# Attention heads with maxima first, split row products, single banks and a reciprocal in quarters

## The chip, the cores and the metric

The kernel runs on one core of one Trainium2 chip. The metric is the device time of one execution in microseconds (us); the median of 3 runs of the kernel before is 5199.88 us (5199.38 to 5200.64).

PE is TensorE (PEld its weight loads), DVE is VectorE, ACT is ScalarE, POOL is GpSimd. PSUM has 8 banks of 128 x 512 f32; products land there, and DVE and ACT read them.

## The reference, cut to what matters

Eight layers run one after the other on x of 2048 tokens and 512 features. The change touches the fifth, a softmax attention over the 2048 tokens as one sequence:

```
q = (x @ Wq.T + bq) * cos(rot);  k = (x @ Wk.T + bk) * sin(rot);  v = x @ Wv.T + bv    # 16 heads of 32
scores = q @ k.T / sqrt(32) * spiral_weight[head]
attn   = softmax(scores, axis=-1)
out    = (attn @ v) @ Wo.T + bo
```

The kernel takes the maximum of each row of scores, adds its negative to the scores, takes the exponential, and divides the product with v by the sum of the exponentials.

## The kernel before, in words

`attention_heads` (tiles named attc) begins when q, k and v are in SBUF. Heads are handled in DT = 4 groups of QH = 4; the four heads of a group lie in the four groups of 32 partitions of q and k, so that a product of head h uses only rows 32h to 32h+31 of the PE array and products of different heads can run side by side. The 2048 queries of a group are cut into TC = 4 blocks of NB = 512, the keys into TT = 16 pieces of 128. A **unit** U is one piece of keys for one block of queries and all four heads: 16 units make a block, 64 a group (UNITS), 256 all (ALL). Units 192 to 255 (from LAST_GROUP on) are the last group.

In a unit of the first three groups PE does, in two halves (lines 1501 to 1508):

- `scores` of two heads: a row product (L1444, bf16), which writes the negative maxima of the queries into the bank (`ones16` by `rows`), and onto it the product of k and q (L1447, f32, which runs as two passes). The result is keys by queries. There are three banks for it, taken in turn: `score_bank(n)` waits until exponential n-3 is done.
- `maxima` of the other two heads of the **next** group (L1455, f32, two passes): queries by keys, one product of 128 queries and 512 keys for each head. DVE reduces both heads at once (L1558, 128x1024 to 128x2). There are two pairs of banks, 3 and 4, 5 and 6; `take` waits until DVE is done with the use before the last.
- `values` of the unit two before (LAG = 2), one half of the queries: L1468, prob by v, in the four column groups of 32 of the array, all 128 rows. They sum in bank 7 over a block.

ACT takes the four exponentials of a unit (L1534) from the score banks into `prob`, which has NP = 4 slots. Slot U is free again when the values of U-4 are done and its part in the sum of exponentials is taken. That sum is formed by POOL, which adds the prob of units 1 to 13 of a block one by one to `acc` (L1410; in the last group DVE does it, L1595). The last two units of a block and `acc` are summed over the keys on PE (`sums`, L1481: 12 products with `ones`), two units after the block's end. Then DVE takes the reciprocal of 128x512 out of PSUM (L1581) and multiplies `o_raw` by it into q (L1585). `o_raw` is the copy that ACT takes of bank 7 (L1540). At a block's last unit DVE also splits the 64 maxima found (`split_maxima`, L1157 to L1163), PE transposes them two units later (L1490) and DVE copies them into `rows` (L1573).

In the last group there are no maxima; PE does four row products, four score products and the values of 512 queries in one piece.

Each engine works its own list in the order in which the code issues it. Waits are on semaphores; what stands behind a waiting instruction on its engine waits too. The next stage, `atte` (L213), begins when all engines have left this one.

## Time and profile before

| | us |
|---|---|
| median of 3 runs | 5199.88 |
| the profiled execution | 5199.14 |
| its span, first to last instruction | 5197.4 |
| attention heads in it | 1233 to 2225 |
| first three groups (units 0 to 191) | 1236 to 2050 |

Over the whole span PE is busy 90%, DVE 46%, ACT 31%, POOL 32%, and the mean granted clock of TensorE is 0.948. The time of a product in the trace runs from its start to its modelled end; several products in different parts of the array overlap, so the distance between starts tells what one costs, not its duration. "x8" in a row of the timeline is a number of instructions merged in one row. One f32 product shows as two passes.

### The profile page before, as it was taken

The page shows a single profiled execution, that of the slowest core. Times are in us where ns is not written, and L with a number is a line of the kernel's source. Part 1 is how long each engine was busy: PE and PEld are TensorE (multiplying, and loading weights), DVE is VectorE, ACT ScalarE, POOL GpSimd, SP SyncE. Part 2 cuts the span into 40 slices and gives each one's busy share as a digit, 9 for nine tenths or more (in the row PEclk, how much of TensorE's full clock was granted, in tenths as well). Part 3 has the DMA queues.
Part 4 walks back from the last instruction along what each step waited for, and adds up shares of the span by engine and source line. Part 5 has one row for each costly group of instructions (what it writes and reads, how often), then busy time and mean ns, then how long its engine had stood idle before and what let it go on. Part 6 is the DMA issues. An engine that isn't in the chain of part 4 may idle for free. (4 is left out here: it accounts for less than half of the span.)

```text
span 5197.4 us, 65036 instructions
## 1 busy us (share of the span) xinstructions
PE 4674.0 (90%) x25716; PEld 2516.1 (48%) x25716; DVE 2376.8 (46%) x3173; ACT 1612.3 (31%) x2757; POOL 1663.4 (32%) x1050
## 2 busy tenths in 40 slices
PE   7359998899999999978999779999999989789996
PEld 3124443333333333246666446666665654466663
DVE  7865887366666666852222223333333331412222
ACT  5414442202555555822211122222222210222110
POOL 2010001003888887024555311111111110145553
PEclk9679999999999999988999889999999999889998
DMA  2000000100000000036888710000000022468887
GB/s 73 0 15 7 6 0 35 35 1 1 1 1 1 1 1 1 1 124 180 259 257 256 191 63 31 23 31 31 23 29 31 23 85 77 159 187 257 259 258 197
DMA packets 237579, 417.60 MB, mean 80 GB/s; under 512 B 31472, under 2 KB 119536, under 8 KB 237296
## 3 DMA queue, kind: packets, MB, share of 16 engines
q1 hardware_dynamic: 179952, 270.89, 15.5%
q0 software_dynamic: 57344, 142.64, 11.3%
q8 instruction: 213, 3.49, 0.3%
q14 instruction: 70, 0.57, 0.0%
HBM read 297.53 MB, written 115.93 MB: 80 GB/s over the span
## 5 line engine op out<-in xcount | busy, mean ns | idle before, releaser
L2363 PE MATMUL linb_pr_ps<-lin_z,linb_wt 128*128 128x512 f32 x1536 | 677.6, 594 | 17.0 <-POOL linb_slope_own L2333 17.0
L1534 ACT ACTIVATE attc_prob<-attc_ps 128x512 f32<-128x512 f32 x1024 | 549.0, 596 | 425.8 <-PE attc_ps L1447 376.6
L1410 POOL TENSOR_TENSOR attc_acc<-attc_acc,attc_prob 128x2048 f32<-128x2048 f32 x144 | 651.7, 4525 | 68.6 <-ACT attc_prob L1534 51.1
L1558 DVE TENSOR_REDUCE attc_peak<-attc_ps 128x2 f32<-128x1024 f32 x384 | 469.7, 1226 | 256.8 <-PE attc_ps L1455 256.8
L1447 PE MATMUL attc_ps<-att_q,att_k 32*128 32x512 f32 x2048 | 528.7, 612 | 0.0
L2363 PEld LDWEIGHTS linb_pr_ps<-lin_z,linb_wt 128*128 128x128 f32 x1536 | 286.2, 191 | 342.5 <-issue 324.5
L1455 PE MATMUL attc_ps<-att_k,att_q 32*128 32x512 f32 x1536 | 443.7, 654 | 2.9 <-DVE attc_tot L1581 2.9
L2340 POOL TENSOR_TENSOR linb_sq<-linb_osb 128x512 f32<-128x512 f32 x64 | 70.1, 1096 | 1039.4 <-ACT linb_osb L2466 1039.4
L2539 DVE SCALAR_TENSOR_TENSOR linb_gated<-linb_osb,linb_norm_w,linb_proj 128x512 f32<-128x512 f32 x64 | 94.4, 1475 | 668.0 <-ACT linb_osb L2466 668.0
L1468 PE MATMUL attc_ps<-attc_prob,att_v 128*32 128x256 f32 (+1 forms) x3472 | 318.2, 439 | 0.3 <-ACT attc_prob L1534 0.3
L1074 DVE TENSOR_TENSOR_SCAN ssmb_state<-ssmb_decay,ssmb_bu 128x2048 f32<-128x2048 f32 x64 | 280.8, 4413 | 54.3 <-PE ssmb_y_ps L927 29.4
L2048 POOL DMA_INDIRECT residual_rows<-moe2c_ye,moe2w_index x128 | 201.8, 1576 | 230.7 <-DVE moe2c_ye L2171 200.7
L2048 POOL DMA_INDIRECT residual_rows<-moe1c_ye,moe1w_index x128 | 201.6, 1575 | 230.2 <-DVE moe1c_ye L2171 200.8
L2449 ACT ACTIVATE linb_proj<-linb_pr_ps 128x512 f32<-128x512 f32 x192 | 114.7, 597 | 517.0 <-PE linb_pr_ps L2363 517.0
L1444 PE MATMUL attc_ps<-att_rows,attc_ones 32*128 32x512 bf16 x1024 | 248.4, 391 | 25.2 <-ACT attc_prob L1534 23.3
L927 PE MATMUL ssmb_y_ps<-ssmb_state,ssmb_diag 128*128 128x512 f32 x512 | 235.0, 606 | 19.5 <-DVE ssmb_y L1083 9.9
L2359 PE MATMUL linb_pr_ps<-linb_wt,lin_z 128*128 128x128 f32 x2048 | 233.8, 275 | 0.0
L2081 PE MATMUL moe2c_gu_ps<-moe2c_xt,moe2w_wgu 128*128 128x256 f32 x1024 | 233.6, 382 | 0.0
L2081 PE MATMUL moe1c_gu_ps<-moe1c_xt,moe1w_wgu 128*128 128x256 f32 x1024 | 233.5, 382 | 0.0
L2359 PEld LDWEIGHTS linb_pr_ps<-linb_wt,lin_z 128*128 128x128 f32 x2048 | 231.2, 192 | 0.5 <-issue 0.5
L783 POOL MEMSET ffn_nothing<- 128x512 f32 x2 | 1.1, 525 | 715.9 <-POOLq L61 715.9
L1468 PEld LDWEIGHTS attc_ps<-attc_prob,att_v 128*32 128x32 f32 x3472 | 68.6, 108 | 332.5 <-ACT attc_prob L1534 179.6
(439 smaller groups left out, 7482.7 us busy)
## 6 DMA issues: line engine op xcount, KB each, us to landing
moe1w_wgu<-in_L_ffn_gate_up_proj SPq DMA_DIRECT2D x32, 1536.0 KB
moe2w_wgu<-in_L_ffn_gate_up_proj SPq DMA_DIRECT2D x32, 1536.0 KB
moe1w_wd<-in_L_ffn_down_proj SPq DMA_DIRECT2D x32, 512.0 KB
gated_features<-linb_gated SPq DMA_DIRECT2D x64, 256.0 KB, 2.3
moe2w_wd<-in_L_ffn_down_proj SPq DMA_DIRECT2D x32, 512.0 KB
linc_gt<-gated_features SPq DMA_DIRECT2D x7, 2048.0 KB, 8.2
linb_wt<-in_L_attn_b_qkv_w SPq DMA_DIRECT2D x16, 768.0 KB, 4.6
residual_rows<-residual SPq DMA_DIRECT2D x8, 1024.0 KB, 4.3
```

Of the source, the lines that this page charges most:

```text
L1074: V.tensor_tensor_scan(state[:, s % RING, :], decay[:, s % RING, :], bu[:, e % 2, :], 0.0, ALU.mult, ALU.add).then_inc(state_done, 1)
L1410: pool.tensor_tensor(acc[:, n % 2, :, :], before, prob[:, U % NP, :, :], ALU.add).then_inc(pool_done, 2 if at == 1 else 1)
L1444: nc.tensor.matmul(ps[:, banks[-1], :], ones16[own, :], rows[own, cols], start=True, stop=False)
L1447: nc.tensor.matmul(ps[:, bank, :], k[own, f, keys], q[own, f, cols], start=False, stop=True).then_inc(s_done, 1)
L1455: last = nc.tensor.matmul(ps[:, bank + h % 2, :], q[own, f, i * P:(i + 1) * P], k[own, f, b * NB:(b + 1) * NB], start=True, stop=True)
L1468: last = nc.tensor.matmul(o_bank[h * DH:(h + 1) * DH, cols], v[:, i, at:at + DH], prob[:, U % NP, h, cols], start=(i == 0), stop=(i == TT ...
L1534: nc.scalar.activation(prob[:, U % NP, h, :], ps[:, n % 3 if at < 0 else at % 6, :], ACT.Exp).then_inc(exp_done, 1)
L1558: V.tensor_reduce(peak[:, w // TT % 2, i % QH, 2 * hp:2 * hp + 2, b], ps[:, bank:bank + 2, :], axis=AX.X, op=ALU.max).then_inc(mx_used, 1)
L2048: pool.indirect_dma_start(out=g.y_dram[x], out_offset=bass.IndirectOffsetOnAxis(ap=index[:, n // 2, n % 2:n % 2 + 1], axis=0), in_=ye[:, y ...
L2081: last = nc.tensor.matmul(gu_ps[:, x, part, :], wgu[:, j % PW, x, k, part * IN:part * IN + P], xt[:, j % 2, x, k, :], start=(k == 0), stop ...
L2359: last = nc.tensor.matmul(pr_ps[:, use % 2, c * CH:(c + 1) * CH], z[:, k, (t * TQ + c) * CH:(t * TQ + c + 1) * CH], wt[:, b, kind, k, :], ...
L2363: last = nc.tensor.matmul(pr_ps[:, use % 2, :], wt[:, b, kind, k, :], z[:, k, t * NB:(t + 1) * NB], start=(k == 0), stop=(k == DT - 1))
```

## The change

Four things change in `attention_heads`; in what is computed nothing changes.

1. **Order on PE** in a unit of the first three groups: maxima of heads 2 and 3, row products of heads 0 and 1, their score products, row products of heads 2 and 3, first half of the values; then maxima of heads 0 and 1, score products of heads 2 and 3, second half of the values. The row products have a function of their own (`heads_in`).
2. **Banks.** Four score banks (0 to 3) instead of three. Maxima, transposed rows and sums take single banks 4, 5, 6 in turn: `take` waits until the use three before is read. Each head's maxima have their own semaphore step and their own reduce on DVE (128x512 to 128x1).
3. **Sum of the exponentials.** POOL (DVE in the last group) adds the 14 units of a block in two halves of seven into two accumulators, of three in turn: 12 adds instead of 13. PE's `sums` has 16 products instead of 12.
4. **Division.** ACT copies the sums out of PSUM into `tot` behind its copy of bank 7. DVE takes the reciprocal in four quarters of 128 columns and multiplies in four, one such step in each of eight units, which begin with the unit behind the sums.

The core of the diff (in `add`, `sums`, `rows_out`, `split` only the names of banks and counts change):

```diff
+        HALF = 7
-        acc = L.sb("acc", [P, 2, QH, NB])
-        tot = L.sb("tot", [P, NB])
+        acc = L.sb("acc", [P, 3, QH, NB])
+        tot = L.sb("tot", [P, 2, NB])
...
-            got = ["A", "B"] if f < DT - 1 else []
+            got = [("peak", h) for h in (2, 3, 0, 1)] if f < DT - 1 else []
...
-        def use_banks(U, kind):
-            if U >= LAST_GROUP:
-                return 6
-            return 3 + 2 * (use_at[U, kind] % 2)
+        def use_bank(U, use):
+            return 6 if U >= LAST_GROUP else 4 + use_at[U, use] % 3
...
+        def accumulator(n, half):
+            return acc[:, (2 * n + half) % 3, :, :]
...
-                    if at == 0:
+                    if at % HALF == 0:
                         continue
...
+                    if at == HALF + 1 and n >= 1:
+                        pool.wait_ge(z_done, n)
...
-            def take(U, kind):
-                n = use_at[U, kind]
-                if U >= LAST_GROUP:
-                    pe.wait_ge(mx_used, n)
-                elif n >= 2:
-                    pe.wait_ge(mx_used, n - 1)
-                return use_banks(U, kind)
+            def take(U, use):
+                n = use_at[U, use]
+                before = n if U >= LAST_GROUP else max(n - 2, 0)
+                if others_upto[before]:
+                    pe.wait_ge(mx_used, others_upto[before])
+                if sums_upto[before]:
+                    pe.wait_ge(z_out, sums_upto[before])
+                return use_bank(U, use)
 
             def score_bank(n):
-                if n < QH * LAST_GROUP:
-                    if n >= 3:
-                        pe.wait_ge(exp_done, n - 2)
-                    return n % 3
                 at = n - QH * LAST_GROUP
-                if at < 3:
-                    pe.wait_ge(exp_done, n - 2)
+                if at < 4:
+                    if n >= 4:
+                        pe.wait_ge(exp_done, n - 3)
+                    return n % 4
...
+            def maxima(U, heads):
                 f, w = U // UNITS + 1, U % UNITS
                 i, b = w // TC, w % TC
-                bank = take(U, kind)
                 for h in heads:
+                    bank = take(U, ("peak", h))
                     own = slice(h * DH, (h + 1) * DH)
-                last.then_inc(mx_done, 1)
+                    nc.tensor.matmul(ps[:, bank, :], q[own, f, i * P:(i + 1) * P], k[own, f, b * NB:(b + 1) * NB],
+                                     start=True, stop=True).then_inc(mx_done, 1)
...
-                sources = [prob[:, (n - 1) % NP, :, :], prob[:, n % NP, :, :], acc[:, n // TT % 2, :, :]]
+                sources = [prob[:, (n - 1) % NP, :, :], prob[:, n % NP, :, :], accumulator(n // TT, 0), accumulator(n // TT, 1)]
...
                 if U < LAST_GROUP:
+                    maxima(U, (2, 3))
+                    heads_in(U, (0, 1))
                     scores(U, (0, 1))
-                    maxima(U, "A", (2, 3))
+                    heads_in(U, (2, 3))
                     if U >= LAG and (U - LAG) % TT:
                         values(U - LAG, 0)
+                    maxima(U, (0, 1))
                     scores(U, (2, 3))
-                    maxima(U, "B", (0, 1))
                     if U >= LAG:
                         values(U - LAG, 1 if (U - LAG) % TT else None)
...
                 nc.scalar.copy(o_raw[:, n % 2, :], o_bank).then_inc(o_out, 1)
+                act.wait_ge(z_done, n + 1)
+                nc.scalar.copy(tot[:, n % 2, :], ps[:, use_bank(n * TT + TT - 1 + LAG, ("sums", 0)), :]).then_inc(z_out, 1)
...
+            def divide(n, step):
+
                 f, t = n // TC, n % TC
-                V.tensor_tensor(q[:, f, t * NB:(t + 1) * NB], o_raw[:, n % 2, :], tot[:, :], ALU.mult).then_inc(o_used, 1)
+                cols = slice(step % QH * P, (step % QH + 1) * P)
+                part = tot[:, n % 2, cols]
+                if step < QH:
+                    dve.wait_ge(z_out, n + 1)
+                    V.reciprocal(part, part).then_inc(inverted, 1)
+                else:
+                    dve.wait_ge(inverted, QH * n + step - QH + 1)
+                    dve.wait_ge(o_out, n + 1)
+                    V.tensor_tensor(q[:, f, t * NB:(t + 1) * NB][:, cols], o_raw[:, n % 2, cols], part, ALU.mult).then_inc(o_used, 1)
...
+                if U < LAST_GROUP and U % TT == TT - 1:
+                    split(U)
+                since = U - LAG - TT
+                if since >= 0 and since % TT < 2 * QH and since // TT < ALL // TT:
+                    divide(since // TT, since % TT)
```

PE's list before: unit 17, the sums of the first block, and the start of unit 18 (L1444 are row products, L1447 score products, L1455 maxima, L1468 values, L1481 sums):

```order
L1444 MATMUL attc_ps<-att_rows,attc_ones 128x512 x2
L1447 MATMUL attc_ps<-att_q,att_k 128x512 x2
L1455 MATMUL attc_ps<-att_k,att_q 128x512 x2
L1468 MATMUL attc_ps<-attc_prob,att_v 32x256 x4
L1444 MATMUL attc_ps<-att_rows,attc_ones 128x512 x2
L1447 MATMUL attc_ps<-att_q,att_k 128x512 x2
L1455 MATMUL attc_ps<-att_k,att_q 128x512 x2
L1468 MATMUL attc_ps<-attc_prob,att_v 32x256 x4
L1481 MATMUL attc_ps<-attc_prob,attc_ones 32x512 x8
L1481 MATMUL attc_ps<-attc_acc,attc_ones 32x512 x4
L1444 MATMUL attc_ps<-att_rows,attc_ones 128x512 x2
L1447 MATMUL attc_ps<-att_q,att_k 128x512 x2
```

The same stretch on PE now (L1470 are maxima, L1454 row products, L1462 score products, L1482 values, L1495 sums):

```order
L1470 MATMUL attc_ps<-att_k,att_q 128x512 x2
L1454 MATMUL attc_ps<-att_rows,attc_ones 128x512 x2
L1462 MATMUL attc_ps<-att_q,att_k 128x512 x2
L1454 MATMUL attc_ps<-att_rows,attc_ones 128x512 x2
L1482 MATMUL attc_ps<-attc_prob,att_v 32x256 x4
L1470 MATMUL attc_ps<-att_k,att_q 128x512 x2
L1462 MATMUL attc_ps<-att_q,att_k 128x512 x2
L1482 MATMUL attc_ps<-attc_prob,att_v 32x256 x4
L1495 MATMUL attc_ps<-attc_prob,attc_ones 32x512 x8
L1495 MATMUL attc_ps<-attc_acc,attc_ones 32x512 x8
L1470 MATMUL attc_ps<-att_k,att_q 128x512 x2
L1454 MATMUL attc_ps<-att_rows,attc_ones 128x512 x2
```

Maxima now stand at the head of each half, two row products have moved ahead of the first values, and the sums have four products more.

DVE's list before, from unit 17 on, behind the sums of the first block (L1581 is the reciprocal, L1585 the multiplication, L1558 the reduces of two heads, L1573 the copy of the rows):

```order
L1581 RECIPROCAL attc_tot<-attc_ps 128x512
L1585 TENSOR_TENSOR att_q<-attc_o_raw,attc_tot 128x512
L1558 TENSOR_REDUCE attc_peak<-attc_ps 128x2 x2
L1573 COPY att_rows<-attc_ps 128x512
L1558 TENSOR_REDUCE attc_peak<-attc_ps 128x2 x26
```

The same place on DVE now, from unit 16 on (L1575 are the reduces of one head, L1591 the copy of the rows, L1602 quarters of the reciprocal, L1606 of the multiplication):

```order
L1575 TENSOR_REDUCE attc_peak<-attc_ps 128x1 x12
L1591 COPY att_rows<-attc_ps 128x512
L1602 RECIPROCAL attc_tot<-attc_tot 128x128
L1575 TENSOR_REDUCE attc_peak<-attc_ps 128x1 x4
L1602 RECIPROCAL attc_tot<-attc_tot 128x128
L1575 TENSOR_REDUCE attc_peak<-attc_ps 128x1 x4
L1602 RECIPROCAL attc_tot<-attc_tot 128x128
L1575 TENSOR_REDUCE attc_peak<-attc_ps 128x1 x4
L1602 RECIPROCAL attc_tot<-attc_tot 128x128
L1575 TENSOR_REDUCE attc_peak<-attc_ps 128x1 x4
L1606 TENSOR_TENSOR att_q<-attc_o_raw,attc_tot 128x128
L1575 TENSOR_REDUCE attc_peak<-attc_ps 128x1 x4
```

One reciprocal ahead of two reduces has become four, each behind the four reduces of a unit, and the multiplications follow in the four units after.

## Rows read from the trace of the kernel before

**Rows 1.** Windows of one block: busy time (instructions) by engine, granted clock, DMA share, GB/s.

```profile
1310.60:1378.70 68.10, 65.84 (x600) 22.38 (x596) 44.86 (x39) 35.23 (x66) 58.85 (x14) 0.97 0.00 1
```

**Rows 2.** Timeline of a steady unit: start, us, engine, line, work, count, idle before.

```profile
1404.38 0.64 PE L1468 MATMUL attc_ps<-attc_prob,att_v 128*32 128x256 f32 x8
...
1404.95 0.59 PE L1444 MATMUL attc_ps<-att_rows,attc_ones 32*128 32x512 bf16 x2
...
1405.70 0.59 PE L1455 MATMUL attc_ps<-att_k,att_q 32*128 32x512 f32 x2
1405.81 0.59 PE L1447 MATMUL attc_ps<-att_q,att_k 32*128 32x512 f32 x1
...
1406.33 0.64 PE L1468 MATMUL attc_ps<-attc_prob,att_v 128*32 128x256 f32 x8
1406.49 1.23 DVE L1558 TENSOR_REDUCE attc_peak<-attc_ps 128x2 f32<-128x1024 f32 x1 [0.72 <-PE attc_ps L1455]
...
1406.90 0.45 PE L1444 MATMUL attc_ps<-att_rows,attc_ones 32*128 32x512 bf16 x2
...
1407.12 0.66 PE L1447 MATMUL attc_ps<-att_q,att_k 32*128 32x512 f32 x2
...
1407.55 0.66 PE L1447 MATMUL attc_ps<-att_q,att_k 32*128 32x512 f32 x2
...
1408.14 0.64 PE L1468 MATMUL attc_ps<-attc_prob,att_v 128*32 128x256 f32 x8
```

**Rows 3.** Timeline of POOL, first three groups.

```profile
1310.61 4.53 POOL L1410 TENSOR_TENSOR attc_acc<-attc_prob 128x2048 f32<-128x2048 f32 x1 [3.12 <-ACT attc_prob L1534]
...
1392.44 51.20 POOL L1410 TENSOR_TENSOR attc_acc<-attc_acc,attc_prob 128x2048 f32<-128x2048 f32 x11 [2.96 <-ACT attc_prob L1534]
...
1989.57 4.53 POOL L1410 TENSOR_TENSOR attc_acc<-attc_prob 128x2048 f32<-128x2048 f32 x1 [3.11 <-issue]
```

**Rows 4.** Timeline of ACT around a block's end, then of DVE.

```profile
1370.99 1.08 ACT L1534 ACTIVATE attc_prob<-attc_ps 128x512 f32<-128x512 f32 x2 [1.62 <-POOL attc_acc L1410]
...
1375.66 1.08 ACT L1534 ACTIVATE attc_prob<-attc_ps 128x512 f32<-128x512 f32 x2 [1.77 <-POOL attc_acc L1410]
...
1381.99 1.09 ACT L1534 ACTIVATE attc_prob<-attc_ps 128x512 f32<-128x512 f32 x2 [2.96 <-PE attc_ps L1447]
...
1389.47 1.08 ACT L1534 ACTIVATE attc_prob<-attc_ps 128x512 f32<-128x512 f32 x2 [4.58 <-PE attc_ps L1447]
...
1380.76 3.36 DVE L1581 RECIPROCAL attc_tot<-attc_ps 128x512 f32<-128x512 f32 x1 [1.89 <-PE attc_ps L1481]
```

**Rows 5.** Timeline of PE at the same place.

```profile
1384.17 1.13 PE L1455 MATMUL attc_ps<-att_k,att_q 32*128 32x512 f32 x4 [0.29 <-DVE attc_tot L1581]
```

**Rows 6.** Timeline of the stage before: maxima and their reduce.

```profile
1031.52 1.14 PE L1243 MATMUL attb_mx_ps<-att_k,att_q 32*128 32x512 f32 x8
...
1032.70 2.36 DVE L1304 TENSOR_REDUCE attb_peak<-attb_mx_ps 128x2 f32<-128x1024 f32 x2 [1.22 <-PE attb_mx_ps L1243]
```

**Rows 7.** Lines of DVE in the stage: line, form, count, busy us, mean ns, idle before.

```profile
L1558 DVE TENSOR_REDUCE attc_peak<-attc_ps 128x2 f32<-128x1024 f32 x384 | 469.7, 1226 | 256.8 <-PE attc_ps L1455 256.8
...
L1581 DVE RECIPROCAL attc_tot<-attc_ps 128x512 f32<-128x512 f32 x16 | 53.7, 3356 | 25.1 <-PE attc_ps L1481 25.1
L1161 DVE CAST att_negp<-attc_neg 128x16 bf16<-128x16 f32 x12 | 11.5, 955 | 0.4
L1585 DVE TENSOR_TENSOR att_q<-attc_o_raw,attc_tot 128x512 f32<-128x512 f32 x16 | 11.1, 692 | 0.6
...
L1157 DVE TENSOR_REDUCE attc_neg<-attc_peak 128x16 f32<-128x64 f32 x12 | 2.6, 220 | 0.4
```

**Rows 8.** Timeline of PE in the last group: values of 512 queries.

```profile
2150.05 1.07 PE L1468 MATMUL attc_ps<-attc_prob,att_v 128*32 128x512 f32 x8
```

**Rows 9.** Timeline of ACT, then PE, at the last group's start.

```profile
2054.68 2.07 ACT L1534 ACTIVATE attc_prob<-attc_ps 128x512 f32<-128x512 f32 x4 [2.34 <-POOL attc_acc L1410]
...
2062.55 0.38 PE L1490 MATMUL attc_ps<-ident,att_negp 128*128 128x128 bf16 x4 [2.83 <-DVE attc_tot L1581]
```

More of the change, by code:

```diff
@@ L1434, in score_bank, with bank_of, heads_in @@
                 return at % 6
+            def bank_of(n):
+                at = n - QH * LAST_GROUP
+                return n % 4 if at < 0 else at % 6
+            def heads_in(U, heads):
+                f, w = U // UNITS, U % UNITS
+                cols = slice(w // TT * NB, (w // TT + 1) * NB)
+                for h in heads:
+                    bank = score_bank(QH * U + h)
+                    own = slice(h * DH, (h + 1) * DH)
+                    nc.tensor.matmul(ps[:, bank, :], ones16[own, :], rows[own, cols], start=True, stop=False)
             def scores(U, heads):
@@ L1439, in scores @@
                 keys, cols = slice(i * P, (i + 1) * P), slice(t * NB, (t + 1) * NB)
[L1440 removed]
                 for h in heads:
[L1442 removed]
                     own = slice(h * DH, (h + 1) * DH)
[L1444 to L1449 removed]
+                    nc.tensor.matmul(ps[:, bank_of(QH * U + h), :], k[own, f, keys], q[own, f, cols], start=False, stop=True).then_inc(s_done, 1)
+            def maxima(U, heads):
                 f, w = U // UNITS + 1, U % UNITS
                 i, b = w // TC, w % TC
[L1452 removed]
                 for h in heads:
+                    bank = take(U, ("peak", h))
                     own = slice(h * DH, (h + 1) * DH)
[L1455 to L1457 removed]
+                    nc.tensor.matmul(ps[:, bank, :], q[own, f, i * P:(i + 1) * P], k[own, f, b * NB:(b + 1) * NB],
+                                     start=True, stop=True).then_inc(mx_done, 1)
             def values(U, half):
@@ L1486, in turn_rows @@
                 pe.wait_ge(neg_done, rows_block(U) + 1)
-                bank = take(U, "R")
+                bank = take(U, ("rows", 0))
                 to = ps[:, bank, :].bitcast(BF16)[:, 0:NB].rearrange("p (i c) -> p i c", c=P)
@@ L1511, in _ @@
                     if U < ALL:
+                        heads_in(U, range(QH))
                         scores(U, range(QH))
                     values(U - LAG, None)
-                for kind in uses_of(U):
-                    if kind == "F":
-                        sums(U, kind)
-                    elif kind == "R":
+                for kind, _ in uses_of(U):
+                    if kind == "sums":
+                        sums(U)
+                    elif kind == "rows":
                         turn_rows(U)
@@ L1533, in exponentials @@
                     act.wait_ge(s_done, n + 1)
-                    nc.scalar.activation(prob[:, U % NP, h, :], ps[:, n % 3 if at < 0 else at % 6, :], ACT.Exp).then_inc(exp_done, 1)
+                    nc.scalar.activation(prob[:, U % NP, h, :], ps[:, n % 4 if at < 0 else at % 6, :], ACT.Exp).then_inc(exp_done, 1)
             def output(n):
```

108 lines of the change are left out of this document (43 added, 65 removed).

## The prediction, made before the changed kernel ran

> **What bounds the kernel now.** The change lies in one stage, the attention heads, so I read the windows view of that stage first [rows 1]: from 1310.60 to 1378.70 us, one block of 16 units, PE is busy 65.84 of 68.10 us, DVE 44.86, ACT 35.23, POOL 58.85. PE sets the pace by its order of work, but "busy" counts products that run side by side in the four groups of 32 rows of the array, so what the order costs must be read from starts. The timeline of one steady unit shows it [rows 2]: the value products start at 1404.38, 1406.33 and 1408.14, so a unit takes 3.76 us in halves of 1.95 and 1.81. A half is: row products, 0.22 to the score products (1406.90 to 1407.12); two passes of a score product, 0.43 each (1407.12, 1407.55); 0.52 from the start of the last pass to the values (1405.81 to 1406.33), which need all rows of the array, that is 0.43 and 0.09 of switching; values 0.57 (1404.38 to 1404.95). The longer half waits for a bank: its row products span 0.59 (1404.95) instead of 0.45 (1406.90), because the exponential that frees the third score bank ends late.
>
> Second, POOL's rows [rows 3]: its first adds of ten blocks stand from 1310.61 to 1989.57, so a block takes 67.9 us. Sixteen steady units would be 60.2. The missing 7.7 stand in ACT's and DVE's rows around a block's end [rows 4]: the exponentials wait for POOL twice (1.62 at 1370.99 and 1.77 at 1375.66; the step between them is 4.67 instead of 3.76, both together cost some 1.7); the sums then cost 2.6 (1375.66 to 1381.99 is 6.33); and the step 1381.99 to 1389.47 is 7.48, 3.7 too long: the reciprocal of 3.36 stands on DVE ahead of the next maxima, and PE's maxima wait for its bank until 1384.17 [rows 5].
>
> **The change, part by part.** I call the first load of the maxima of head 0 in a unit H, and count from there.
>
> *Product order.* Work between two value stretches, by the same row spacings: first half, groups of heads 2 and 3 hold maxima (0.53 to the second pass when the load is not hidden: in the earlier stage four products side by side take 1.14 from the first load to the last end [rows 6], of which 0.59 is a second pass and 0.02 the spread; then 0.43) and row products (0.22); heads 0 and 1 have row products and scores beside them. With 0.09 and values 0.57 it is 1.84; I take 1.83. Second half: 0.53 + 0.43 + 0.09 + 0.57 = 1.62, since its row products were done before. Without waits a unit would take 3.45, 0.31 less than now: 0.14 is the bank wait (four score banks instead of three), the rest mostly the 0.22 of row products out of the second half.
>
> *Banks of the maxima.* Now there are three single banks instead of two pairs, and the k-th use waits for use k-3. So head 3 of a unit waits until DVE has reduced head 0 of the unit before, whose product is issued only in that unit's second half. This is a new loop: maxima product 0.53 + 0.59 = 1.12; to the reduce 0.04 (in the earlier stage maxima end at 1032.66 and the reduce starts at 1032.70 [rows 6]); the reduce of 128x512, which no row shows: from 1.226 for 1024 columns and 0.220 for 64 [rows 7], 1.05 ns a column, 0.69; back to PE 0.05 (1384.12 to 1384.17 [rows 4, 5]); a second wait instruction in front of each such product, between 0 and 0.05, taken as 0.04. That is 1.94 after H; PE is free at 1.62. From head 3's load to the next H 1.83. The loop is 3.77 us, as long as the unit now: the gain of the order goes into this wait. Behind head 3's load stand on PE the row products and scores of heads 0 and 1, and ACT waits for those.
>
> Here the Trainium skill has a rule (TensorE: Matmul & The Clock Gate, The mechanism): matmuls start and end in program order. The trace bears out the end: now the reduce starts at 1406.49 [rows 2], 0.20 after the maxima's own last pass ends (1405.70 + 0.59) but just behind the score pass issued before it (1405.81 + 0.59 = 1406.40); in the changed order nothing unfinished stands ahead of head 0's maxima, so 0.04 is right. Were the 0.20 kept, the sum would be 5184. The trace is against the start: see rival C.
>
> *DVE.* Four single reduces are 2.8 a unit instead of 2.45; nothing waits, as DVE is free for over 1 us of 3.77. Reciprocal: a quarter of 3.356 is 0.84 [rows 7], and the fixed part of a DVE instruction, 0.15 by the two reduces there, has to be paid once more: 0.95, one a unit, between head 1's reduce and head 2's. It makes head 2's reduce end at H + 3.95 and head 1 of the next unit wait some 0.25; that ends inside the 0.32 that head 3 waits anyway. Cost 0, bounds 0 and 0.3 in 4 units of 16. The multiplications (0.7 / 4 and a fixed part) hide likewise. The splitting of maxima (0.22 and 0.96 [rows 7] and a third, short instruction) delays head 2's reduce by some 1.5, which after the same slack leaves 0.7 a block.
>
> *POOL.* Twelve adds instead of 13 in a block: 51.20 for 11 [rows 3] is 4.66 each, 55.9; the gap of 2.96 before the third add goes with the long step, some 1.2 stays before the second, and the one at the block's start falls from 3.12 to 2.3, since four score banks let four exponentials run together. POOL needs 59.4, less than PE: its two waits (1.7) go.
>
> *Sums.* Four more products, eight passes, are two rounds of 0.43 in the four column groups: sums 3.44 instead of 2.58. ACT's copy of the sums (0.59) is over before head 0's maxima of the next unit need the bank; after a sum head 3 doesn't wait.
>
> A block: 14 units at 3.77 = 52.8; the unit with the sums 3.45 + 3.44; the unit behind it 3.12 without a first value stretch (two row stretches joined, 2.03, then 0.09 and the full values, 1.07 with their latency [rows 8], 1.00 without) and 0.35 of transposes, 3.47; splitting 0.7; small waits of DVE behind the row copy 0.1: 64.0. Against 67.9 this is -3.9, 11 times: -43. First block, no sums, slower clock at its start: -1.5. Start of the last group: the waits for POOL (2.34) and for the reciprocal (2.83) [rows 9] go, of the former the part beyond the usual wait, the sums add: -2.7. Last group: 0.86 in each of three further sums and in the last, together +3.4; DVE has one add less a block there, which makes room for the quarters of the reciprocal. After the last sum: copy 0.6, four reciprocals 3.8, four multiplications 1.1, against 3.36 + 0.69 now [rows 7]: +1.5. Sum -42.3. The profiled execution took 5199.14 (span 5197.4), 0.7 below the median 5199.88; forecast **5157**.
>
> **Rivals.** A: the drain loop doesn't bind (PE takes the wait late, or two reduces overlap more). The unit is 3.45, a block 59.5 by PE, 59.4 by POOL, in fact some 59.8: -8.1 x 11, and 13 units in the first block at -0.3: 5107. For it: each link is 0.05 to 0.1 uncertain. Against: the use waited for is only three back, and 0.32 of slack would have to be found in the chain.
>
> B: the loop is longer, the reduce starts 0.20 after its product as in [rows 2]. Unit 3.93, block 66.2, -1.7 x 11: 5184. For it: that is the latency shown in this stage. Against: rows 6.
>
> C, slower: PE starts products of different row groups only in program order. That is the Trainium skill's rule in the section named above. Then the row products of heads 0 and 1 would start with head 3's second pass, 0.43 later than I count; the first half grows by 0.43, the unit to 4.20, the block to 70.9: +3.0 x 11 and 4 in the first block, 5239. Against: the last score pass (1405.81) starts after the maxima's last passes (1405.70) [rows 2], though all score products are issued before the maxima. Any mechanism makes the kernel slower only from a unit of 4.02 on (42 us over 167 units is 0.25).
>
> **Chances.** Forecast 0.60 (5135 to 5176: unit 3.65 to 3.88), A 0.13, B 0.16, C 0.06, and 0.05 for no gain, 5205, if both DVE bounds (0.3 four times, 0.7 more at splitting, 1.9 x 11 = 21) add to B. A difference under 0.2%, 10.4 us, can't be told from none. Faster: 0.60 + 0.13 + two thirds of B = 0.84; within 0.2% 0.10; slower 0.06, which is C. Range 5106 to 5192: A to B with DVE's bounds.
>
> **What would show it.** Right: a unit of about 3.77 with PE or its loads waiting 0.3 for the reduce (L1575) once a unit and no longer for the exponential; a block of 64; no wait of ACT for POOL; single reduces of 0.69; the step behind the sums near 3.5 instead of 7.5. Wrong: units of 3.45 with POOL as releaser (A), a reduce that starts 0.2 after its maxima (B), row products that start only 0.5 after the maxima's load (C), or DVE without idle time in the units with reciprocals.

## The result, and the profile after

The changed kernel takes 5208.6 us, the kernel before 5200.3 (medians of 20 runs each, taken in turns; spread 5202.9 to 5212.1 and 5197.9 to 5203.0). The ratio is 1.0016, with an interval of 1.0010 to 1.0022: 8 us slower, inside the 0.2% (10.4 us) that I had called no change, though the interval does not include 1. I had forecast 5157 and a range up to 5192, so the time is outside. The execution that the hardware profiler took has a span of 5208.2 us, against 5197.4 before.

The stage can be cut at three places: where its first exponential, the first of unit 16 and the first of unit 192 start. ACT's timeline at these three places, of the kernel before:

```profile
1236.20 1.09 ACT L1534 ACTIVATE attc_prob<-attc_ps 128x512 f32<-128x512 f32 x2 [1.38 <-PE attc_ps L1447]
...
1302.90 0.60 ACT L1534 ACTIVATE attc_prob<-attc_ps 128x512 f32<-128x512 f32 x1 [1.60 <-POOL attc_acc L1410]
...
2050.28 0.60 ACT L1534 ACTIVATE attc_prob<-attc_ps 128x512 f32<-128x512 f32 x1 [1.62 <-PE attc_ps L1447]
```

and of the changed kernel:

```profile
1236.93 0.60 ACT L1551 ACTIVATE attc_prob<-attc_ps 128x512 f32<-128x512 f32 x1 [1.40 <-PE attc_ps L1462]
...
1295.91 0.60 ACT L1551 ACTIVATE attc_prob<-attc_ps 128x512 f32<-128x512 f32 x1 [0.95 <-PE attc_ps L1462]
...
2057.76 0.60 ACT L1551 ACTIVATE attc_prob<-attc_ps 128x512 f32<-128x512 f32 x1 [1.29 <-PE attc_ps L1462]
```

From these starts: the first block took 66.7 us and takes 59.0 (-7.7; forecast -1.5). The eleven blocks behind it took 747.4 and take 761.9 (+14.5; forecast -43). From there to the first product of the output projection it was 175.2 (2225.48) and is 175.7 (2233.46), where I had forecast +2.2 for the three terms together. So nearly all that is wrong stands in the eleven blocks: 69.3 us each instead of 64.0.

Yet the steady unit is what I forecast. Its timeline, to be held against [rows 2] (PEld are the loads of PE's weights):

```profile
1427.54 1.29 DVE L1575 TENSOR_REDUCE attc_peak<-attc_ps 128x1 f32<-128x512 f32 x2 [0.81 <-PE attc_ps L1470]
...
1428.02 0.96 PE L1470 MATMUL attc_ps<-att_k,att_q 32*128 32x512 f32 x2
1428.29 0.09 PEld L1454 LDWEIGHTS attc_ps<-att_rows,attc_ones 32*128 32x128 bf16 x2
...
1428.98 0.64 PE L1454 MATMUL attc_ps<-att_rows,attc_ones 32*128 32x512 bf16 x2
...
1429.55 0.64 PE L1482 MATMUL attc_ps<-attc_prob,att_v 128*32 128x256 f32 x8
...
1430.12 0.19 PEld L1470 LDWEIGHTS attc_ps<-att_k,att_q 32*128 32x128 f32 x2 [0.41 <-DVE attc_peak L1575]
...
1430.65 0.59 PE L1470 MATMUL attc_ps<-att_k,att_q 32*128 32x512 f32 x2
...
1431.19 0.64 PE L1482 MATMUL attc_ps<-attc_prob,att_v 128*32 128x256 f32 x8
1431.28 0.69 DVE L1575 TENSOR_REDUCE attc_peak<-attc_ps 128x1 f32<-128x512 f32 x1 [0.81 <-PE attc_ps L1470]
```

Head 2's maxima start at 1428.02. Head 3's load waits for the first of the two reduces, over at 1427.54 + 0.69 = 1428.23, and what is queued behind it (row products of heads 0 and 1) is loaded at 1428.29. Then the values start at 1429.55. The second half, 1429.55 to 1431.19, is 1.64 (forecast 1.62). The last pass of its maxima ends at 1430.65 + 0.59 = 1431.24, and the reduce starts 0.04 later (forecast 0.04). The starts of the exponentials of such units are 3.74 apart (forecast 3.77).

What is long are single units. Two kinds recur in each block. The first stands in the eighth unit of a block, here on POOL, DVE, PE and ACT:

```profile
1392.54 13.84 POOL L1418 TENSOR_TENSOR attc_acc<-attc_acc,attc_prob 128x2048 f32<-128x2048 f32 x3
1410.08 4.54 POOL L1418 TENSOR_TENSOR attc_acc<-attc_prob 128x2048 f32<-128x2048 f32 x1 [3.70 <-issue]
...
1398.76 3.11 DVE L1606 TENSOR_TENSOR att_q<-attc_o_raw,attc_tot 128x128 f32<-128x128 f32 x1
1404.73 1.80 DVE L1606 TENSOR_TENSOR att_q<-attc_o_raw,attc_tot 128x128 f32<-128x128 f32 x1
1409.96 0.28 DVE L1606 TENSOR_TENSOR att_q<-attc_o_raw,attc_tot 128x128 f32<-128x128 f32 x1
...
1402.53 0.70 PE L1470 MATMUL attc_ps<-att_k,att_q 32*128 32x512 f32 x1 [1.27 <-DVE attc_peak L1575]
...
1404.16 1.09 ACT L1551 ACTIVATE attc_prob<-attc_ps 128x512 f32<-128x512 f32 x2 [3.40 <-PE attc_ps L1462]
```

The same instruction, one quarter of a multiplication, takes 3.11, 1.80 and 0.28 us. POOL's three adds end at 1392.54 + 13.84 = 1406.38, the second of them some 4.65 earlier, at 1401.7; the two long multiplications end at 1401.87 and 1406.53, each 0.15 behind an add. The third runs in POOL's gap of 3.70. Behind the first, the maxima's reduces are late, PE waits for a bank, and ACT for PE: in this block, the third, the step between the first exponentials of its eighth and ninth unit is 7.45 instead of 3.74 (5.9 to 8.3 over the blocks). In all, 45 multiplications and casts take over 0.5 us: all 12 casts, and three of the four multiplications in each of eleven blocks. Each of the 45 began while an add of POOL ran, and ends 0.06 (casts) or 0.15 us (multiplications) behind the end of that add.

The second kind follows the splitting of the maxima. Its longest case, on POOL, DVE, PE and ACT:

```profile
1285.38 13.84 POOL L1418 TENSOR_TENSOR attc_acc<-attc_acc,attc_prob 128x2048 f32<-128x2048 f32 x3
...
1295.37 3.91 DVE L1161 CAST att_negp<-attc_neg 128x16 bf16<-128x16 f32 x1
...
1300.16 0.72 PE L1470 MATMUL attc_ps<-att_k,att_q 32*128 32x512 f32 x1 [2.66 <-DVE attc_peak L1575]
...
1301.82 1.08 ACT L1551 ACTIVATE attc_prob<-attc_ps 128x512 f32<-128x512 f32 x2 [4.82 <-PE attc_ps L1462]
```

A cast of 16 numbers a partition ends at 1299.28, the adds at 1299.22. The exponentials of this unit begin at 1295.91 and those of the next at 1304.75, 8.84 later; in the other blocks this step is 4.5 to 5.1. The view of lines gives the sums over the stage, to be held against [rows 7]:

```profile
L1575 DVE TENSOR_REDUCE attc_peak<-attc_ps 128x1 f32<-128x512 f32 x768 | 491.9, 682 | 195.2 <-PE attc_ps L1470 194.1
...
L1606 DVE TENSOR_TENSOR att_q<-attc_o_raw,attc_tot 128x128 f32<-128x128 f32 x64 | 74.9, 1179 | 0.0
L1602 DVE RECIPROCAL attc_tot<-attc_tot 128x128 f32<-128x128 f32 x64 | 60.1, 943 | 9.0 <-ACT attc_tot L1559 7.2
L1161 DVE CAST att_negp<-attc_neg 128x16 bf16<-128x16 f32 x12 | 19.9, 1658 | 0.4
```

The multiplications were 11.1 us in 16 instructions and are 74.9 in 64; the casts were 11.5 and are 19.9. Reduces (0.68) and reciprocals (0.94) stand as forecast, beside the same adds.

### The profile page after: what moved, and what is told of

The parts are those of the page before. It is cut to its first block and busy times, and to the rows that moved or that the text cites. A ratio compares the mean times of both kernels' runs of the same rounds, so it can differ in the third digit from the quotient of the medians.

```text
span 5208.2 us, 66496 instructions
## 1 busy us (share of the span) xinstructions
PE 4693.8 (90%) x25844; PEld 2545.0 (49%) x25844; DVE 2452.1 (47%) x3649; ACT 1621.8 (31%) x2773; POOL 1608.5 (31%) x1038
## 5 line engine op out<-in xcount | busy, mean ns | idle before, releaser
L1575 DVE TENSOR_REDUCE attc_peak<-attc_ps 128x1 f32<-128x512 f32 x768 | 491.9, 682 | 195.2 <-PE attc_ps L1470 194.1
L1418 POOL TENSOR_TENSOR attc_acc<-attc_acc,attc_prob 128x2048 f32<-128x2048 f32 x120 | 542.8, 4524 | 42.1 <-ACT attc_prob L1551 26.6
L1470 PE MATMUL attc_ps<-att_k,att_q 32*128 32x512 f32 x1536 | 524.1, 656 | 20.2 <-DVE attc_peak L1575 18.6
L1462 PE MATMUL attc_ps<-att_q,att_k 32*128 32x512 f32 x2048 | 503.7, 629 | 0.0
L1482 PE MATMUL attc_ps<-attc_prob,att_v 128*32 128x256 f32 (+1 forms) x3472 | 316.1, 437 | 0.3 <-ACT attc_prob L1551 0.3
L1470 PEld LDWEIGHTS attc_ps<-att_k,att_q 32*128 32x128 f32 x1536 | 168.8, 188 | 212.7 <-DVE attc_peak L1575 104.3
L2613 PE MATMUL linc_y_ps<-linc_wt,linc_gt 128*128 128x512 f32 x512 | 222.2, 597 | 0.1
```

The costliest lines, as they stand in the source:

```text
L1418: pool.tensor_tensor(to, before, prob[:, U % NP, :, :], ALU.add).then_inc(pool_done, 2 if at % HALF == 1 else 1)
L1462: nc.tensor.matmul(ps[:, bank_of(QH * U + h), :], k[own, f, keys], q[own, f, cols], start=False, stop=True).then_inc(s_done, 1)
L1470: nc.tensor.matmul(ps[:, bank, :], q[own, f, i * P:(i + 1) * P], k[own, f, b * NB:(b + 1) * NB], start=True, stop=True).then_inc(mx_done, 1)
L1482: last = nc.tensor.matmul(o_bank[h * DH:(h + 1) * DH, cols], v[:, i, at:at + DH], prob[:, U % NP, h, cols], start=(i == 0), stop=(i == TT ...
L1575: V.tensor_reduce(peak[:, w // TT % 2, i % QH, h, b:b + 1], ps[:, use_bank(U, ("peak", h)), :], axis=AX.X, op=ALU.max).then_inc(mx_used, 1)
```

## The experiments

My theory behind them: on DVE, instructions that cast or that read two inputs from SBUF wait for an add of POOL that is running; reduces and reciprocals don't. Rows carry the line numbers of their own kernel; in the longer ones L1161 and L1606 have moved to L1172 to L1177 and L1618 or L1627. Times are medians, ratios are to the kernel before.

**The multiplication back on POOL.** One multiplication of 128x512 by POOL instead of four by DVE, for blocks 0 to 10. It stands ahead of POOL's seventh add of the next block, the first of the second half. The cut in front of the call leaves out the slice of q that `qs` names.

```diff
+    pool.wait_ge(inverted, QH * n)
+    pool.wait_ge(o_out, n)
...
+    pool.tensor_tensor(qs, o_raw[:, m % 2, :], tot[:, m % 2, :], ALU.mult).then_inc(o_pool, 1)
...
-                else:
+                elif n >= BY_POOL:
                     dve.wait_ge(inverted, QH * n + step - QH + 1)
```

> The changed kernel, but for blocks 0 to 10 POOL does the multiplication by the inverted sums, in one piece of 128x512, ahead of its add of the ninth unit of the next block, where it has a gap of 3.7 us; DVE keeps the quarters of the reciprocal. Theory (DVE's multiplication, which reads two SBUF tensors, waits until POOL's running add ends, up to 4.5 us, and PE's maxima wait behind it): the step from unit 23 to 24 of each block falls from 7.45 to 3.74; POOL's second half begins about 1.2 us later and shifts the cast at the block's end, so 2.5 to 3.7 us a block are gained, 5168 to 5181 us. Rival 1 (the new PE order or the single banks cost the time): no change, 5205 to 5212. Rival 2 (the multiplications wait for the semaphores of the reciprocals): no change or slower.

Measured: 5190.9 us, ratio to before 0.9982 (0.9973 to 0.9991). The long eighth unit is gone (3.74), but less was won than expected, since the casts grew:

```profile
L1161 DVE CAST att_negp<-attc_neg 128x16 bf16<-128x16 f32 x12 | 34.0, 2833 | 0.4
...
1406.36 1.26 POOL L1419 TENSOR_TENSOR att_q<-attc_o_raw,attc_tot 128x512 f32<-128x512 f32 x1
```

The cast is now 2.83 in the mean instead of 1.66: it comes when POOL has more of an add ahead of it. The unit behind it takes 6.0 to 7.5, and 8.8 in the first block that has one. How long these instructions take depends on where in an add they fall: the casts here are those of the changed kernel, with the same 16 numbers.

**One input in place of two.** The multiplications replaced by reciprocals of one of the two inputs; the division by the sums is left out.

```diff
-V.tensor_tensor(q[...][:, cols], o_raw[:, n % 2, cols], part, ALU.mult).then_inc(o_used, 1)
+V.reciprocal(q[...][:, cols], o_raw[:, n % 2, cols]).then_inc(o_used, 1)
```

> The changed kernel, but the four multiplications on DVE are replaced by reciprocals of o_raw into q (one SBUF input instead of two, same place, same waits, same size); the division by the sums is left out. Theory (two inputs from SBUF wait for POOL's add): each such instruction takes 0.95 us and never up to 3.1, the step from unit 23 to 24 falls to 3.74, 3.7 us a block less, 5168 us. Rival 2 (what costs is the place and its waits): the steps stay at 7.45, 5205 to 5212, or more since 0.95 is longer than 0.28.

Measured: 5169.1 us, ratio 0.9940 (0.9925 to 0.9955). POOL's timeline and DVE's at the place where the multiplication took 3.11, then the line's sum:

```profile
1388.43 13.87 POOL L1418 TENSOR_TENSOR attc_acc<-attc_acc,attc_prob 128x2048 f32<-128x2048 f32 x3
1394.68 0.94 DVE L1606 RECIPROCAL att_q<-attc_o_raw 128x128 f32<-128x128 f32 x1
...
L1606 DVE RECIPROCAL att_q<-attc_o_raw 128x128 f32<-128x128 f32 x64 | 59.3, 936 | 0.0
```

In the midst of three adds of POOL an instruction with one input takes 0.94, and all 64 of them take that (mean 0.936). By itself it takes longer than a multiplication that meets no add (0.28), and yet the kernel is 39 us shorter with it (5208.6 to 5169.1).

**Short adds.** POOL adds head 0 only; the sums of the other heads are left out, and the exponentials have a scale of 0.1 so that values stay finite.

```diff
-pool.tensor_tensor(to, before, prob[:, U % NP, :, :], ALU.add)
+pool.tensor_tensor(to[:, 0, :], before[:, 0, :], prob[:, U % NP, 0, :], ALU.add)
```

> The changed kernel with POOL's adds cut to the first head (128x512 instead of 128x2048; the sums of the other heads are left out and the exponential is scaled by 0.1, so that numbers stay finite). Theory: DVE's multiplication waits at most for one add of 1.1 us, so its longest is 1.4 instead of 3.11, and the cast at a block's end at most 1.3 instead of 3.91; the step from unit 23 to 24 falls below 5, a block is 64 to 65 us, 5155 to 5170 us. Rivals 1 and 2: the long step stays, over 5190 us.

Measured, in one execution: 5148.3 us, 60 less than the changed kernel. DVE's lines:

```profile
L1606 DVE TENSOR_TENSOR att_q<-attc_o_raw,attc_tot 128x128 f32<-128x128 f32 x64 | 17.4, 280 | 0.0
...
L1161 DVE CAST att_negp<-attc_neg 128x16 bf16<-128x16 f32 x12 | 2.4, 202 | 0.4
```

With adds of 1.28 us, 15 of a block's 63.7, none of the 76 instructions began while one ran. So this run doesn't show what a short add does to them; it shows that both stalls go when POOL is out of their way.

**Half a reduce.** DVE reduces 256 of the 512 columns (maxima of half the keys left out; scale 0.1 as above).

```diff
-... ps[:, use_bank(U, ("peak", h)), :],
+... ps[:, use_bank(U, ("peak", h)), 0:NB // 2],
```

> The changed kernel with DVE's reduce over 256 of the 512 columns of each maxima product (half of the maxima's search left out; the exponential scaled by 0.1). Theory of the loop (head 3's maxima wait for the reduce of head 0 of the unit before, and this sets the unit): the reduce takes 0.42 instead of 0.69, the steady unit falls from 3.74 to 3.47, some 3.8 us a block; the long step from unit 23 to 24 stays. 5165 to 5175 us. Rival (the PE order by itself sets 3.74): the unit stays at 3.74, 5205 to 5212 us.

Measured, in one execution: 5205.8 us. The steady unit shows the loop as expected, value products of PE two halves apart:

```profile
1418.11 0.64 PE L1482 MATMUL attc_ps<-attc_prob,att_v 128*32 128x256 f32 x8
...
1421.59 0.64 PE L1482 MATMUL attc_ps<-attc_prob,att_v 128*32 128x256 f32 x8
```

1418.11 to 1421.59 is 3.48 instead of 3.74: the reduce went from 0.68 to 0.42, and the unit shrank by all of that 0.26. That confirms that one reduce lies on the chain that sets the unit, as the loop of three banks has it. The total missed its expectation by over 30 us, because multiplications (mean 1.64 instead of 1.18) and casts (3.26) fell earlier into POOL's adds. What the faster unit won was eaten by longer stalls.

**Both stalls taken away.** The multiplication on POOL as in the first experiment, and the split of the maxima by reduces (semaphores and views are left out of the lines).

```diff
-    V.tensor_copy(parts[:, :, :, 0], negs)
-    V.tensor_tensor(parts[:, :, :, 1], negs, parts[:, :, :, 0], ALU.subtract)
+    V.tensor_reduce(parts[:, :, :, 0], neg[:, :, 0:1], axis=AX.X, op=ALU.max)
+    V.tensor_reduce(neg[:, :, 1], parts[:, :, :, 0:1], axis=AX.X, op=ALU.max, negate=True)
+    V.tensor_reduce(parts[:, :, :, 1], neg[:, :, :], axis=AX.X, op=ALU.add)
```

> Both stalls of VectorE taken away: the multiplication by the reciprocals is done by POOL in its own gap (as before), and the splitting of the maxima, which had a cast and a subtraction with two inputs, is written as four reduces with one input each. My theory (only instructions that cast or that read two inputs from SBUF wait for a running add of POOL; reduces and reciprocals don't): the four steps of the split take some 0.2 us each, the unit behind the split shrinks from 4.5 to 7 us to about 3.8, the step with the late multiplications to 3.74, the mean block of 16 units from 69.26 to 63.7 to 64.2, the whole kernel from 5208.6 to 5145 to 5155. Rival (any small instruction of VectorE on SBUF waits while POOL adds): the reduces of the split are drawn out as the cast was, the unit behind it stays above 4.5, the block above 65, the kernel above 5165.

Measured: 5150.2 us, ratio 0.9903 (0.9886 to 0.9921). The window of the second full block, against [rows 1], and the line of the reduce that took the cast's place:

```profile
1365.48:1429.33 63.85, 63.85 (x608) 24.07 (x612) 45.38 (x74) 35.83 (x67) 55.49 (x13) 1.00 0.01 1
...
L1172 DVE TENSOR_REDUCE att_negp<-attc_neg 128x16 bf16<-128x16 f32 x12 | 2.7, 224 | 0.4
```

The block is 63.85, PE is busy in all of it, and the kernel stands 7 us under my forecast of 5157.

**The split by reduces alone.** As above, with the multiplications left on DVE.

> The split of the maxima by four reduces alone; the multiplications stay on VectorE. My theory: the unit behind the split falls from 4.5 to about 3.8 us, while the step with the multiplications stays between 5 and 8.5 us, since these still wait for the running add; the block about 68.4 (from 69.26), the kernel 5190 to 5205. Rival (the cast was what pushed the multiplications into the adds): both stalls go and the kernel takes about 5150.

Measured: 5191.8 us, ratio 0.9986 (0.9977 to 0.9996). The unit behind the split is 3.5 to 3.8; the eighth unit stays at 5.9 to 8.3. Either stall stays when only the other is taken away: 5208.6 goes to 5190.9 without the one, to 5191.8 without the other, and to 5150.2 without both. The sum of the two alone, 35, is less than the 58 of both, as the casts cost more once the multiplications are gone: the unit behind the split takes 5.2 in the mean in the changed kernel and 7.1 in the first experiment, while the eighth unit hardly changes when the casts go (7.4 and 7.0).

**The multiplications in another place.** As the last one, with the same four multiplications on DVE issued together later, at the end of the first unit of the following block.

```diff
-                    divide(since // TT, since % TT)
+                    if since % TT < QH or since // TT >= (DT - 1) * TC - 1:
+                        divide(since // TT, since % TT)
+                if U % TT == 0 and 2 <= U // TT <= (DT - 1) * TC:
+                    for step in range(QH):
+                        divide(U // TT - 2, QH + step)
```

> e6_reduce_split with the four multiplications still on VectorE, but issued together in the first unit of the block after next, where POOL has no add running (in e6 its adds end 0.8 us after a block's first exponential and start again 5.6 us later). My theory (the same instruction waits only for a running add): each takes 0.28 us, no step of 5 us or more but that of the sums, block about 63.8, kernel 5145 to 5155. Rival (two inputs of fp32 from SBUF are slow on VectorE here whatever POOL does): they stay at 1 to 3 us, the block at 66 or more, the kernel above 5175.

Measured: 5149.1 us, ratio 0.9901 (0.9886 to 0.9916).

```profile
1418.87 4.54 POOL L1430 TENSOR_TENSOR attc_acc<-attc_acc,attc_prob 128x2048 f32<-128x2048 f32 x1
1425.37 0.88 DVE L1618 TENSOR_TENSOR att_q<-attc_o_raw,attc_tot 128x128 f32<-128x128 f32 x4
```

POOL's last add of the block is over at 1423.41, and the four take 0.88 together. Of all 64, one still began in an add and took 0.97; the others take about 0.28. The same instructions on the same engine with the same data cost 43 us less for being issued elsewhere: it is neither their work nor their engine. The only long one of the 64 is the one that met an add.

**The kernel before, with the split by reduces.**

> The kernel before with the split of the maxima by four reduces, nothing else. My theory (the cast waits for the running add of POOL there too, 0.99 against 0.20 us in the earlier stage, where POOL has no such adds): 0.7 to 1.5 us less in each of 11 blocks, 5183 to 5193 us. With e5_both at 5150 that would put the change without its two stalls at 35 to 43 us, near the 42 that I had predicted. Rival (the unit behind the split is long in the kernel before for another reason, the transposes or the wait for them): 5197 to 5201.

Measured: 5200.4 us, ratio 1.0002 (0.9992 to 1.0011). I had expected 5183 to 5193: wrong. The cast did wait there for the end of an add (0.96 mean in [rows 7]; the reduce in its place takes 0.22), but ACT's exponentials wait at the same place for that same add [rows 4] (1.62 before, 1.60 in this run), so nothing hung on the cast. The change took this wait of ACT away, and so uncovered the cast's.

**The row products of heads 2 and 3 behind the first value half.** One of the two moves of the change undone, on the kernel without stalls.

```diff
-                    heads_in(U, (2, 3))
                     if U >= LAG and (U - LAG) % TT:
                         values(U - LAG, 0)
+                    heads_in(U, (2, 3))
                     maxima(U, (0, 1))
```

> e5_both with the row products of heads 2 and 3 put back behind the first half of the value products, as the kernel before had them. My theory (the unit is a loop: from head 3's maxima to the first values, then head 0's maxima, its reduce, and back to head 3's maxima; the row products of heads 2 and 3 lie in the first part, 0.22 us, and would lie beside the second part, which has slack of some 0.3): the steady unit falls from 3.74 to 3.5 to 3.6 us, the block by 14 x 0.18 to about 61.3 and the kernel to some 5115 to 5125. Rival (the row products ahead of the values are worth what the title of the change makes of them, since the second half sets the pace): the unit rises by 0.2 to 3.95 and the kernel takes some 5190.

Measured: 5140.1 us, ratio 0.9884 (0.9867 to 0.9902); its runs (5137.7 to 5140.7) don't overlap those of the kernel with this move (5147.4 to 5150.6). It is the fastest that I ran. The unit on PE:

```profile
1401.51 0.64 PE L1500 MATMUL attc_ps<-attc_prob,att_v 128*32 128x256 f32 x8
1402.08 0.86 PE L1488 MATMUL attc_ps<-att_k,att_q 32*128 32x512 f32 x2
1402.25 0.39 PE L1472 MATMUL attc_ps<-att_rows,attc_ones 32*128 32x512 bf16 x2
...
1402.91 0.59 PE L1480 MATMUL attc_ps<-att_q,att_k 32*128 32x512 f32 x2
1403.43 0.64 PE L1500 MATMUL attc_ps<-attc_prob,att_v 128*32 128x256 f32 x8
```

The unit is 3.67, not the 3.5 to 3.6 expected, and the kernel takes 5140.1 where 5115 to 5125 was expected; the direction is that of my theory and against the rival. From values to values, the first half falls from 2.10 to 1.92 and the second rises from 1.64 to 1.75. That the first half doesn't fall by the full 0.22 of the row products I put down to the row products and scores of heads 0 and 1, queued on PE behind head 3's waiting maxima: they run from 1402.25 to the values at 1403.43. No run tests this. Measured is that the move that issues the row products of heads 2 and 3 earlier costs this kernel 10 us.

**The maxima of heads 2 and 3 behind the scores of heads 0 and 1.** The other move undone, alone and then with the first.

```diff
-                    maxima(U, (2, 3))
                     heads_in(U, (0, 1))
                     scores(U, (0, 1))
+                    maxima(U, (2, 3))
```

> e5_both with the maxima products of heads 2 and 3 put back behind the scores of heads 0 and 1. My theory: those two pairs run in different row groups side by side, and the maxima still wait for the reduce of head 0, so the loop and the unit stay as they are, 3.7 to 3.8 us, and the kernel within 10 us of e5_both; the scores of heads 0 and 1 no longer queue behind the waiting maxima and start some 0.3 us earlier. Rival (the maxima's load is on the path and is now issued later): the unit rises by 0.1 to 0.4 us, the kernel by 20 to 60 us.

Measured, in one execution: 5157.7 us, 7.5 more than with the maxima first; the unit is 3.75 as expected, and the unit of the sums and the next are 0.2 longer each.

> e5_both with both moves of the products undone: scores of heads 0 and 1 ahead of the maxima of 2 and 3, and the row products of heads 2 and 3 behind the first value half. My theory from e7's trace: there the first half is set by head 3's maxima, which wait for the reduce, and the row products and scores of heads 0 and 1 queued behind it (2.31 to 3.48, 1.18 us), longer than the maxima themselves (1.05); put ahead they are out of the way, the unit falls from 3.67 to 3.5 to 3.6 us, but the unit of the sums and the one behind it grow by 0.2 each as in e8: block 60.5 to 62.3, kernel 5115 to 5135. Rival (as e8 beside e5_both: the order of these two does nothing for the unit): block 63.3 to 63.6, kernel 5143 to 5150.

Measured, both undone: 5156.3 us, ratio 0.9915 (0.9901 to 0.9929). I expected 5115 to 5135: wrong. The unit is 3.75, since the second half became the long one:

```profile
1402.15 0.64 PE L1500 MATMUL attc_ps<-attc_prob,att_v 128*32 128x256 f32 x8
...
1402.73 1.05 PE L1488 MATMUL attc_ps<-att_k,att_q 32*128 32x512 f32 x2
1403.09 0.70 PE L1480 MATMUL attc_ps<-att_q,att_k 32*128 32x512 f32 x2
...
1404.15 0.64 PE L1500 MATMUL attc_ps<-attc_prob,att_v 128*32 128x256 f32 x8
```

1402.15 to 1404.15 is 2.00, where the second half takes 1.75 with the maxima of heads 2 and 3 first and the row products behind (the run that took 5140.1). Head 3's maxima are issued later, so their reduce is, and the next pair's second load waits for its bank: that is my reading of the starts (the scores behind it at 1403.09, 0.36 behind the first maxima). No run took this wait away. The maxima first are worth 16 us where the row products are behind (5156.3 to 5140.1), the row products ahead cost 10 where the maxima are first. In the other two pairings the same moves are worth less: the maxima first 7.5 where the row products are ahead (one execution), the row products ahead about nothing where the maxima are behind (5156.3 to 5157.7, one execution). Both moves together win 6 (5156.3 to 5150.2).

## Why the prediction was wrong

The step that failed is in the paragraph on DVE: "The multiplications (0.7 / 4 and a fixed part) hide likewise." I priced them from a row where they were 0.69 for 512 columns [rows 7], and with nothing beside it one of 128 columns indeed takes 0.28. But in the kernel before all 16 stand where POOL has no add running, and I moved that price to a place where one does. They took up to 3.1 us each, 74.9 in all, where 64 of 0.28 are 17.9. With the neighbouring term they cost the kernel 58 us (5208.6 less 5150.2), more than the whole miss of 52.

That neighbour is the term for the splitting, 0.7 a block. Its row already showed 0.955 us for a cast of 16 numbers a partition, where a reduce over 64 took 0.220 [rows 7]. I took this as the cast's own time. Most of it was a wait: where no add runs it takes 0.202 (short adds). I had both numbers and didn't ask why the smaller job was the longer one.

The mechanism: an instruction of DVE that casts, or reads two inputs from SBUF, does not end before the add of POOL that was running when it began. In the thirteen traces 60 casts and 100 multiplications of this stage began in such an add; every cast ended 0.06 us behind it and every multiplication 0.14 to 0.15. Shorter adds, an instruction with one input, and another place each take the stall away with little else changed. Two inputs as such are not enough: in the output projection, DVE's additions with one input in SBUF and one in PSUM began in 68 cases while an addition of POOL ran, and took 0.69 as the others did. The Trainium skill has this rule (SBUF — State Buffer, Who interferes with whom): the two engines share a port pair that is locked for a whole instruction, casts can contend for it and instructions with two SBUF inputs do against one of POOL that reads SBUF, reduces never. This case's rows agree: 3.11, 1.80 and 3.91 us for the former, 0.68 and 0.94 for reduces and reciprocals beside the same adds. By the same section the lock works both ways, by who comes first; that can't be seen here. In the kernel before, the subtraction behind each of the 12 casts begins 0.05 ahead of POOL's next add and ends 0.18 into it, and these adds take 4.52 to 4.54 like the rest. It was the rule to weigh in the prediction, and I weighed another. The multiplications, if issued at a random moment of adds that take 4.53 of each 4.65 us, wait some 2.2 us each (an estimate: 4.53 / 4.65 of half an add); four of them a block, less the 1 us that I counted as free on DVE in each unit, are some 5 us, more than the 3.9 that I had won in a block. That was a rival on the slower side, and my prediction doesn't name it.

The rest, by the prediction's steps:

- *The unit.* Loop of three banks 3.77 forecast, 3.74 measured; its links 0.04 and 0.69 measured as 0.04 and 0.68. Halving the reduce confirmed the loop. I wrote that the gain of the order goes into this wait; in fact one of the two moves loses 0.07 a unit.
- *Rivals.* A needed units of 3.45: refuted. B needed a reduce 0.20 behind its product: it is 0.04. C needed row products half a microsecond behind the maxima's load: they are loaded at 1428.29, right behind head 3's. The case of no gain, 5205, came nearest to the time, but by luck: it has DVE's bounds of 0.3 and 0.7 in it, where 3.7 (eighth unit) and up to 5.1 (split) were measured, and B's unit.
- *The block.* 64.0 forecast, 63.85 without the stalls, partly by luck: the unit behind the sums is 4.29 instead of 3.47, the splitting by reduces takes 0.04 where 0.7 was forecast for the cast.
- *The sums.* The step with them 6.89 forecast, 6.97 measured.
- *POOL.* ACT's waits for it nearly went, as forecast: from 42.6 us in 30 waits to 6.0 in 6 between 1310 and 2050. That very thing uncovered the cast.
- *The end.* Four reciprocals 3.8 and four multiplications 1.1 forecast, 3.4 and 0.8 measured; DVE's timeline behind the last sums:

```profile
2228.52 3.39 DVE L1602 RECIPROCAL attc_tot<-attc_tot 128x128 f32<-128x128 f32 x4 [7.25 <-ACT attc_tot L1559]
2231.82 0.83 DVE L1606 TENSOR_TENSOR att_q<-attc_o_raw,attc_tot 128x128 f32<-128x128 f32 x4
```

- *The first block.* -1.5 forecast, -7.7 measured, a miss in the other direction (last section).

## What to carry to other kernels

Before an instruction is moved, look at what runs beside it in its old place and in the new one, on the engines that share something with it; its duration in a row holds only for the old neighbours. A row whose time doesn't fit its size (0.96 us for 16 numbers beside 0.22 for 64) can hold a wait, and a wait that is hidden today is uncovered by the change that removes its cover. And an order of issue can only be judged on the chain that sets the unit: here, without the stalls, one move won 16 us and the other then cost 10, so that the whole reordering won 6.

## What the runs showed that I had not expected

The granted clock at the stage's start. Windows of 4 us (busy time and count of PE, its loads, DVE, ACT, POOL, then the clock), first of the kernel before, then of the changed one:

```profile
1230.00:1234.00 4.00, 0.75 (x8) 0.49 (x10) 1.95 (x5) 0.47 (x1) 0.27 (x2) 0.70 0.00 0
...
1238.00:1242.00 4.00, 3.75 (x19) 0.91 (x11) 1.23 (x1) 1.37 (x3) 0.00 (x0) 0.50 0.00 0
...
1246.00:1250.00 4.00, 3.75 (x18) 0.89 (x10) 1.23 (x2) 1.09 (x3) 4.00 (x1) 0.50 0.00 0
```

```profile
1238.00:1242.00 4.00, 3.99 (x27) 1.74 (x21) 2.86 (x5) 2.19 (x5) 0.00 (x0) 0.84 0.00 0
1242.00:1246.00 4.00, 4.00 (x35) 1.57 (x33) 3.70 (x6) 3.12 (x6) 2.48 (x1) 1.00 0.00 0
```

Both kernels begin the stage at 0.50 of the clock, 1.2 GHz, behind a stretch in which PE did little (0.75 of 4 us). The kernel before stayed there until about 1252; the changed one was at 2.4 GHz from about 1239. What stands out in PE's rows is that before, up to 1248, it had an idle gap in every half unit, for the third score bank, here the row

```profile
1242.37 0.60 PE L1444 MATMUL attc_ps<-att_rows,attc_ones 32*128 32x512 bf16 x1 [0.25 <-ACT attc_prob L1534]
```

and with four banks there is none until the clock has risen. The first three units took 17.1 us and take 10.3; these 6.8 are nearly all of the 7.7 that the first block won. All eleven kernels here with four score banks have the early rise, with either order of products (first blocks of 57.3 to 59.7 us), and neither of the two with three has it (66.7). No run changes the gaps alone, so that they are what held the clock down is not shown.

The multiplication of 128x512 takes POOL 1.26 us, where it took DVE 0.69. On POOL it is still as good as on DVE in POOL's gap (5150.2 and 5149.1), and far better than on DVE beside the adds (5191.8).
